# Five gather layers of a graph network on one core: the last four full blocks in chunks of four tiles

## What is computed

```python
x = layernorm(x + L0(x))   # degree-scaled segment sum of h[src]
x = layernorm(x + L1(x))   # two convolutions: segment max of x[src] @ W_msg + edge_attr @ W_edge
x = layernorm(x + L2(x))   # softmax aggregation (sums of exp(m) and of m * exp(m)) over x[src]
x = layernorm(x + L3(x))   # attention over x[src], with a self loop, then tanh
```

## Time and profile before

| what | value |
|---|---|
| median of 3 runs | 3746.14 us (3744.34 to 3748.51) |
| the profiled execution, its own time | 3745.6 us |
| its span | 3743.8 us |
| busy: POOL | 2679.4 us (72%) |
| busy: DVE | 2813.2 us (75%) |
| busy: ACT | 1864.7 us (50%) |
| busy: PE | 1770.4 us (47%) |
| gathers of layers 1a, 1b, 2, 3 (391 each) | 380.8, 381.1, 388.4, 373.5 us busy |
| scatters of layer 3 (392) | 384.7 us busy |

### The profile page before, as it was taken

One profiled execution on the slowest core, in us unless ns is written; L12 is line 12 of the kernel. 1 busy time (PEld: TensorE's weight loads), 2 busy tenths in 40 slices (PEclk: granted clock), 3 DMA queues, 4 the chain that ended last, 5 costly groups with the idle time before them and its releaser, 6 DMA issues. The chain is left out here.

```text
span 3743.8 us, 39744 instructions
## 1 busy us (share of the span) xinstructions
PE 1770.4 (47%) x8382; PEld 1287.8 (34%) x8382; DVE 2813.2 (75%) x10541; ACT 1864.7 (50%) x3815; POOL 2679.4 (72%) x2760
## 2 busy tenths in 40 slices
PE   5478675888766666644544426778710000000000
PEld 2244313777654555532222226767600000000000
DVE  8899987888876666658999968888865556555565
ACT  8699702677662222224555447777733333333333
POOL 7377776777747777757777657777567777777776
PEclk9799855888887777766666657777755555555555
DMA  2111297665555666646666635555422222222221
GB/s 54 50 40 40 68 291 208 176 167 158 156 144 187 204 212 205 203 132 203 208 203 203 199 127 191 191 191 191 158 83 83 73 83 77 79 82 74 83 75 54
DMA packets 380540, 524.64 MB, mean 140 GB/s; under 512 B 221915, under 2 KB 255984, under 8 KB 380043
## 3 DMA queue, kind: packets, MB, share of 16 engines
q1 hardware_dynamic: 286154, 366.89, 29.5%
q0 software_dynamic: 94144, 155.21, 17.6%
HBM read 230.36 MB, written 291.54 MB: 139 GB/s over the span
## 5 line engine op out<-in xcount | busy, mean ns | idle before, releaser
L1626 POOL DMA_INDIRECT l_G<-t,src x391 | 388.4, 993 | 148.6 <-issue 118.8
L1932 POOL DMA_INDIRECT l_G<-t,src x391 | 373.5, 955 | 158.7 <-issue 107.4
L1307 POOL DMA_INDIRECT l1a_G<-t,src x391 | 380.8, 974 | 147.2 <-issue 116.7
L1307 POOL DMA_INDIRECT l1b_G<-t,src x391 | 381.1, 975 | 142.7 <-issue 117.7
L1947 POOL DMA_INDIRECT out<-O,nidx x392 | 384.7, 981 | 127.8 <-issue 118.8
L2166 PE MATMUL l_psR<-l_diag,l_ones 128*128 128x128 f32 x2 | 0.8, 500 | 991.9 <-DVE l_diag L2030 991.9
L642 POOL DMA_INDIRECT O<-x_pad,nidx x344 | 326.3, 949 | 104.7 <-issue 104.7
L973 POOL DMA_INDIRECT l_G<-xs,src x327 | 310.8, 950 | 99.7 <-issue 97.5
L2166 PEld LDWEIGHTS l_psR<-l_diag,l_ones 128*128 128x128 f32 x2 | 0.5, 310 | 992.0 <-DVE l_diag L2030 992.0
L207 ACT ACTIVATE O<-O,l_shift,l_rstd 128x96 f32<-128x96 f32 x784 | 291.4, 455 | 27.7 <-DVE l_shift L201 26.5
L1480 PE MATMUL l1b_psE<-l1b_G,ident 128*128 128x384 f32 (+1 forms) x198 | 149.5, 858 | 264.4 <-DMA l1b_G<-t,src 264.4
(11 more groups left out here) (351 smaller groups left out, 6291.8 us busy)
## 6 DMA issues: line engine op xcount, KB each, us to landing
h<-l_G SPq DMA_DIRECT2D x96, 392.0 KB, 2.9
t<-l1b_t_out SPq DMA_DIRECT2D x48, 768.0 KB
h<-l_G SPq DMA_DIRECT2D x48, 768.0 KB, 3.5
xs<-en_y SPq DMA_DIRECT2D x48, 392.0 KB, 4.2
t<-l_t_out SPq DMA_DIRECT2D x48, 392.0 KB
l_H<-t SPq DMA_DIRECT2D x48, 392.0 KB, 3.2
en_y<-x_pad SPq DMA_DIRECT2D x48, 384.0 KB, 5.0
t<-l_tr_out SPq DMA_DIRECT2D x48, 384.0 KB
```

Source lines behind the costliest of these rows:

```text
L1307: pool.indirect_dma_start(tile(c)[:, q, :], None, table, bass.IndirectOffsetOnAxis(k.src[:, at:at + 1], 0))\
L1626: pool.indirect_dma_start(tile(c)[:, q, :], None, table, bass.IndirectOffsetOnAxis(k.src[:, at:at + 1], 0))\
L1932: pool.indirect_dma_start(tile(c)[:, q, :], None, t4, bass.IndirectOffsetOnAxis(k.src[:, at:at + 1], 0))\
```

## The change

SPLIT = 4: the last four full blocks (44 to 47) become two chunks of 4 tiles each. The chunks 0 to 43 stay 8 wide, 44 to 51 are 4 wide, 52, 53 and 54 are the 4, 2 and 1 tiles of the last block, and 55 is `F`. TAIL = NL - 2 = 53 takes the place of NCH wherever NCH counted chunks. Semaphores that belonged to a slot (`kept`, `gathered`) now belong to a half of a slot, and a chunk waits for the chunk that held its own tiles (`holder`). In layer 1 a narrow chunk loads only its half of the edge attributes.

```diff
+HALF = Q // 2
+SPLIT = 4
-STARTS = [b * Q for b in range(NCH - 1)] + [NCH * Q - 8, NCH * Q - 4, NCH * Q - 2, K, K + 1]
+STARTS = [b * Q for b in range(NCH - 1 - SPLIT)]
+STARTS += [b * Q + h for b in range(NCH - 1 - SPLIT, NCH - 1) for h in (0, HALF)]
+STARTS += [NCH * Q - 8, NCH * Q - 4, NCH * Q - 2, K, K + 1]
 NL = len(STARTS) - 2
+TAIL = NL - 2
...
+def place_of(c, slots):
+    return STARTS[c] // Q % slots, STARTS[c] % Q // HALF
+
+def holder(tile):
+    return max(c for c in range(NL) if STARTS[c] <= tile)
...
+class Places:
+    def __init__(self, sem, name, slots):
+        self.slots = slots
+        self.sems = {(s, h): sem(f"{name}{s}_{h}") for s in range(slots) for h in range(2)}
+    def of(self, c):
+        return self.sems[place_of(c, self.slots)]
+    def among(self, c, first=0):
+        return [i for i in range(first, c + 1) if place_of(i, self.slots) == place_of(c, self.slots)]
+    def stores(self, c):
+        return 16 * len(self.among(c))
+    def last_stores(self):
+        lasts = {place_of(c, self.slots): c for c in range(TAIL - 1)}
+        return [(self.of(c), self.stores(c)) for c in lasts.values()]
...
 class Landed:
-        self.slots = [k.sem(f"{name}_gathered{s}") for s in range(slots)]
-        self.late = [k.sem(f"{name}_late{c}") for c in range(NCH, NL)]
+        self.places = Places(k.sem, f"{name}_gathered", slots)
+        self.late = [k.sem(f"{name}_late{c}") for c in range(TAIL, NL)]
...
 def entering(step):
-    return range(NCH - 1, NL) if step == NCH - 1 else range(step, min(step + 1, NCH - 1))
+    return range(TAIL - 1, NL) if step == TAIL - 1 else range(step, min(step + 1, TAIL - 1))
...
@@ layer1, SP @@
             def load(c):
-                for h in range(2) if c < NCH else []:
-                    if c >= 1:
-                        sp.wait_ge(edged, 2 * (c - 1) + h + 1)
-                    sp.dma_start(edge[:, h, :], edge_k[c, h]).then_inc(edge_in[h], 16)
+                block, half = divmod(STARTS[c], Q)
+                for h in (half // HALF,) if TAIL - 1 > c >= NCH - 1 - SPLIT else range(2) if c < TAIL else ():
+                    if block >= 1:
+                        sp.wait_ge(edged, 2 * (block - 1) + h + 1)
+                    sp.dma_start(edge[:, h, :], edge_k[block, h]).then_inc(edge_in[h], 16)
...
@@ the gathers of layers 1, 2 and 3, and in the same way of layer 0 @@
-                s = c % SLOTS
-                if SLOTS <= c < NCH:
-                    pool.wait_ge(joined, c - SLOTS + 1)
-                    pool.wait_ge(chained, c - SLOTS + 2)
-                    pool.wait_ge(kept[s], 16 * (c // SLOTS))
+                if STARTS[c] >= SLOTS * Q:
+                    held = holder(STARTS[c] - SLOTS * Q)
+                    pool.wait_ge(joined, held + 1)
+                    pool.wait_ge(chained, held + 2)
+                    pool.wait_ge(kept.of(held), kept.stores(held))
...
@@ layer1, PE @@
-                if first:
-                    if 1 <= c < NCH:
-                        pe.wait_ge(added, c)
-                else:
-                    if WAYS <= c < NCH:
-                        pe.wait_ge(chained, c - WAYS + 1)
+                if WAYS * Q <= STARTS[c] < K:
+                    pe.wait_ge(added if first else chained, holder(STARTS[c] - WAYS * Q) + 1)
+                if not first:
                     pe.wait_ge(gathered.of(c), gathered.by(c))
...
@@ layer3, POOL @@
             for t in range(NL + 3):
-                for c in range(NCH - 1, NL) if t == NCH - 1 else range(t, min(t + 1, NCH - 1)):
+                for c in entering(t):
                     gather(c)
-                if t == NCH:
+                if t == TAIL:
                     head()
                 if t >= 2:
                     scatter(t - 2)
```

More of the change, by code:

```diff
@@ L148, in select_head @@
     dve.drain()
-    for c in range(NCH - 1, NL):
+    for c in range(TAIL - 1, NL):
         for q in range(width(c)):
@@ L859, in layer0 @@
     SLOTS = 4
-    HALF = Q // 2
     ctx = ExitStack()
@@ L894, in layer0 @@
         placed = [k.sem(f"l0_placed{c}") for c in range(LATE, NCH + 1)]
-        kept = [sem(f"kept{s}") for s in range(SLOTS)]
+        kept = Places(sem, "kept", SLOTS)
         headed = k.sem("l0_headed")
@@ L975, in _ @@
                         .then_inc(gathered.of(c), 16)
-            for s in range(SLOTS):
-                pool.wait_ge(kept[s], 16 * kept_before(s, SLOTS))
+            for stored_sums, count in kept.last_stores():
+                pool.wait_ge(stored_sums, count)
             pool.indirect_dma_start(F[:, 0, :], None, hist, bass.IndirectOffsetOnAxis(k.hrow[:, 0:1], 0))\
@@ L1054, in _ @@
                     factors(t - 1)
-                if t == NCH - 1:
-                    for c in range(NCH, NL):
+                if t == TAIL - 1:
+                    for c in range(TAIL, NL):
                         chain(c)
-                if t == NCH:
+                if t == TAIL:
                     close()
@@ L1393, in _ @@
             for t in range(LAST + 1):
-                if t < NCH:
+                if t < TAIL:
                     chain(t)
-                if not first and t == NCH - 1:
-                    for c in range(NCH, NL):
+                if not first and t == TAIL - 1:
+                    for c in range(TAIL, NL):
                         chain(c)
@@ L1406, in _ @@
                     join(t)
-                if first and t == NCH - 1:
-                    for c in range(NCH, NL):
+                if first and t == TAIL - 1:
+                    for c in range(TAIL, NL):
                         chain(c)
```

72 lines of the change are left out of this document (35 added, 37 removed).

## The result

The changed kernel takes 3766.46 us, the median of 5 runs (3762.23 to 3767.62), and the kernel before, run beside it, 3744.34 us (3743.87 to 3748.51). The ratio is 1.005, with a 95% interval from 1.0039 to 1.0061: slower by 15 to 23 us. The profiled execution has a span of 3764.7 us; before it was 3743.8.

A forecast was written before the change was run, and what follows sets the result against it. POOL's gather descriptors bound every layer, so only layer ends and layer 3's queue order could move. 8.7 + 2.6 + 7 - 1 - 6 = +11.3 us gave 3757 us; range 3745 to 3769, the forecast's own 3753 to 3762.

The forecast's parts named there:

- the third rival: SP's queue: edge loads cannot keep up with narrow steps, layer 1b +11.5, layer 1a nothing; +21, 3767 us; chance 0.15.
- the gain of layer 1a: Layer 1a's end: halved chunk 47 leaves DVE 3.7 us sooner, PE's product 5.49 becomes 2.75; -6 us, ends -9 and 0.
- the price of layer 0: Layer 0: DVE pays for two halves per block, part returned by shorter waits; +2.6 us, ends +0 and +6.
- Layer 3, +8.7 forecast: POOL's queue in layer 3: eight scatters move ahead of the last seven gathers, 10.2 us, less 1.54 us returned.
- The 1.54 us that should come back: Layer 3, DVE's measuring in the last block's step: 2.54 us for 4 tiles instead of 4.08 for 8.
- The surcharge: Layer 0, DVE: two halves of 5.99 and 4.93 us, together 1.5 us over a 9.38 us full step; four blocks +5.9.
- Layer 1b, +7 forecast: Layer 1b: DVE surcharge 1.66 us a block, less waits returned, +5.1; plus 2 for edge loads; ends +4 and +11.5.
- The 2 us for late edge loads: Layer 1b, SP's queue: eight narrow steps each held 0 to 0.8 us by edge loads, 0 to 6.4, taken as 2.
- Layer 2, -1 forecast: Layer 2: surcharge 5.6 us, against 4.4 us-type gather waits (4 x 1.1) and some 2.2 us returned; ends -5 and +3.
- Narrow steps cost half: Rival: no DVE surcharge, a narrow step costs half a full one, every layer but 3 gains; -10, 3736 us; chance 0.12.
- the semaphores of the halves do nothing: Rival: semaphores by halves never bind, since POOL has no wait for a slot; part of each case, no own chance.
- the figure weighed in the prediction: DVE instruction overhead from the skill: six added instructions cost 0.4 to 0.7 us a block, not 1.5; sum about +2 us.

The follow-up runs named there:

- e3: Changed kernel, all layers split, but POOL's queue in layer 3 in the old order; 3758.96 us, ratio 1.0032.
- e5: Changed kernel with only the last full block of each layer in halves (SPLIT = 1); 3760.03 us, ratio 1.0043.
- e12: e11 with layer 3's gathers each ahead of one more block of scatters, block 48's back at their own step; 3728.22 us, ratio 0.9954.
- e6: Changed kernel with the last eight full blocks of each layer in halves (SPLIT = 8); 3775.37 us, ratio 1.0088.
- e4: Changed kernel with four edge buffers instead of two and edge loads one chunk further ahead in layers 1a and 1b; 3762.0 us, ratio 1.0038.
- e9: e7 without the deeper edge buffers: four blocks split in layer 1a alone, block 48's gathers earlier in layer 3; 3739.45 us, ratio 0.9988.
- e1: Changed kernel with no block split (SPLIT = 0), keeping the semaphores by halves and POOL's longer waits; 3747.57 us, ratio 0.9994.
- e2: Changed kernel with four blocks split in layer 3 alone, none in the other layers; 3756.74 us, ratio 1.0023.
- e7: Changed kernel split (four blocks) in layer 1a alone, deeper edge buffers in 1a and 1b, layer 3 in old order with block 48's gathers earlier; 3737.0 us, ratio 0.9983.
- e11: e7 with eight blocks split in layer 1a instead of four, and the deeper edge buffers in layer 1a only; 3735.38 us, ratio 0.997.

## Why the prediction was right, and where not

The direction, the largest term and the range (3745 to 3769) held; the size of the middle did not. 3757 was forecast and 3766.5 measured, beyond the forecast's own 3753 to 3762. That the range held is in part luck: its upper part was there for the third rival, late edge loads in layer 1b, and the time got there by other terms. Two steps failed: the gain of layer 1a, which was entered in full and did not come (6 us), and the price of layer 0 (3.4 us). In the means of the profiles, layers 0, 1b and 3 with +6.0, +6.0 and +10.3 make up the whole loss of 22 us.

- **Layer 3, +8.7 forecast, +10.3 measured.** The mechanism is shown by e3, e5 and e12. The eight scatters cost 10.7 us up to the score of the 4-tile chunk. The 1.54 us that should come back do: from that score to the next it takes 9.02 us (3716.28 to 3725.30) and took 10.56 before (3694.97 to 3705.53). But 0.5 us is lost again in the stages that follow, and 0.7 behind the last scatter.
- **Layer 0, +2.6 forecast, +6.0 measured** in the means of the profiles, +8.3 between the first two (the means: 7.4 up to the bias of block 48, less 1.4 behind it, where the sum had 1.3; the unsplit time behind it depends on PE's clock, as the last section shows). The surcharge was put at 1.5 us a block and is nearer to 1.9 (11.3 us for a block against 9.38). The waits at the change of width, 2.1 us beyond the ordinary one with four blocks and 2.9 with one, were priced in layer 1b and in layer 2 but left out here, as if DVE, which was short of time, could have no one to wait for. Against this, DVE's waits for gathers gave back some 3 us where 1.99 was entered.
- **Layer 1b, +7 forecast, +6.0 measured**, with a nearly right sum for partly wrong reasons. The ends grow in proportion to the blocks (e5, e6), by 1.5 to 1.7 us each, but DVE's own surcharge is 1.2 us of it, where the prediction had 1.66. The 2 us for late edge loads are 1.1 us of waits for the product, and with loads a chunk earlier the narrow steps took 0.8 us less (e4).
- **Layer 1a, -6 forecast, nothing measured.** Four profiles with the split and two edge buffers, one to four blocks, end after 24.0 to 31.4 us and three unsplit after 24.2 to 29.2. A gain of some 3 us or more exists with the split and edge loads further ahead (17.4 to 21.3 us); whether four split blocks alone bring some of it, profiles and totals do not agree (e9). The prediction named what could take it, PE's product of the next chunk behind a late load, gave it as the end of its range, and then did not count it. Its term for the product was also too large: the 5.49 us of the earlier trace rows are at a granted clock of 0.50, and the same product took 2.87 us at 1.00 (e1, e2), so that halving it saves 2.6 us in the one case and 1.3 in the other.
- **Layer 2, -1 forecast.** Its ends are 43.2 to 48.1 us unsplit and 44.2, 45.9 and 47.2 with four blocks. No difference can be read.
- **The rivals.** "SP's queue holds the narrow steps": in layer 1a its mechanism is there (DVE's 14.2 us of waits for the product, 3.6 with earlier loads, e4), in layer 1b, where most of its price was, it costs 1.1 us; its total, 3767, is the measured one, yet it gets there by other terms. "Narrow steps cost half" is excluded by e6: each further split block costs 0.9 us in layer 0 and 1.6 in layer 1b. That the semaphores of the halves do nothing is shown by e1.

On the surcharge the trace lies above the figure weighed in the prediction. The Trainium skill (Perfetto Trace Analysis, Optimizing Scalar/DVE Operations) has about 60 ns of overhead for a DVE instruction on SBUF and 125 ns on PSUM, from which 0.4 to 0.7 us a block was estimated; the steps of layers 0 and 1b show 1.9 and 1.2 us. The prediction left out what the same passage of the Trainium skill adds: these are busy times, and the latency in a profile is about twice as long. By that the estimate for six instructions that follow one another is 0.7 to 1.5 us, which takes in layer 1b; of layer 0's 1.9 us, 0.37 is a second ordinary wait for ACT. The prediction's sum by that figure, about +2 us, also holds only for its 0.7 us; with 0.4 us it would be -2.

The other sentence of that section of the Trainium skill, that smaller instructions may help where an engine is not saturated but makes bubbles elsewhere, agrees with layer 1a once the edge loads come earlier (17.4 to 21.3 us against 24.2 to 29.2 unsplit).

## What to carry to other kernels

When a loop counts its lag in chunks, making the chunks smaller also makes the lag smaller, and everything that stands in one queue in that order moves: count the lag in bytes or tiles, and ask which of the queue's items the end waits for. Splitting the last pieces of work paid here only on the path whose engines had time to spare, and surely so only where its other inputs came earlier too; where an engine is already full, each halved block costs its surcharge, and the change of width costs waits once. A forecast gain that a known obstacle can take away should not be entered in full. Before two profiles are compared at the end of a layer, look at PE's granted clock in both, and at whether the profiled execution is near the median of its runs.

## What was not expected of the hardware

**The clock of PE at the end of layer 0.** e7 has layer 0 unsplit, as before, and still its end is 40.9 us and not 36.4 to 38.3 as in seven others (e12, unsplit too, has 41.5). Stretches of 5 us (length, busy time of PE, PE's loads, DVE, ACT and POOL, granted clock, DMA share, GB/s), first of before, then of e7:

```profile
1087.90:1092.90 5.00, 4.32 (x26) 3.87 (x27) 4.29 (x27) 3.65 (x10) 0.00 (x0) 0.86 0.61 157
1092.90:1097.90 5.00, 2.94 (x22) 2.30 (x21) 2.97 (x18) 3.98 (x11) 0.00 (x0) 1.00 0.33 78
1097.90:1102.90 5.00, 3.89 (x27) 3.63 (x27) 4.04 (x17) 3.73 (x10) 0.00 (x0) 1.00 0.38 103
```

```profile
1087.80:1092.80 5.00, 4.32 (x14) 4.22 (x14) 4.06 (x26) 3.70 (x11) 0.00 (x0) 0.50 0.53 142
1092.80:1097.80 5.00, 4.65 (x21) 4.20 (x21) 1.87 (x10) 2.53 (x5) 0.00 (x0) 0.50 0.23 53
1097.80:1102.80 5.00, 4.32 (x14) 3.87 (x15) 2.69 (x13) 2.52 (x8) 0.00 (x0) 0.50 0.39 109
```

Before, PE has its full clock (2.4 GHz) there; in e7 it has the lower level (1.2 GHz) for 15 us. The two products with the weights take 5.49 and 5.32 us where before they took 2.87 each, and DVE waits for what PE does behind them, as its timeline of e7 shows:

```profile
1095.76 0.99 DVE L1081 SCALAR_TENSOR_TENSOR O<-l_psN,l_inv,O 128x96 f32<-128x96 f32 x4 [3.12 <-PE l_psN L1189]
...
1105.30 0.54 DVE L1081 SCALAR_TENSOR_TENSOR O<-l_psN,l_inv,O 128x96 f32<-128x96 f32 x2 [1.50 <-PE l_psN L1189]
```

These 4.6 us, in the same code and for no cause that these runs show, are as much as most of the terms that the prediction added up. With split blocks the granted clock was 0.50 from 10 to 5 us before the end of the layer in all five profiles; unsplit it was 0.50 in e12 and 0.76 to 1.00 in the other eight. Yet the time after the bias of block 48 was 21.9 to 22.6 us with split blocks and 21.8 to 26.9 us unsplit, so it is not what makes the split slower.

**The gathers' own time.** From the first gather to the last, layers 1a and 1b took 492.1 to 502.1 us over all profiles, with the same 391 gathers. The length of such a layer from one profile tells nothing under some 5 us; its end tells more, though the same code of layer 1a ended after 17.4 us in e11 and 20.4 in e12, and the totals of many runs tell most. Layer 3 is steadier: 1013.9 and 1014.2 us in before and e1.
